# Replicating the attention values through a scratch in memory: one store and four loads a tile in place of sixteen transfers inside SBUF

## The chip, the core and the metric

One core of one Trainium2 chip runs the whole kernel. The metric is device time in microseconds (us). The engines are named as in the profile: PE (TensorE, matrix products), PEld (its weight loads), DVE (VectorE), ACT (ScalarE), POOL (GpSimd), and SP (SyncE), which here only issues the transfers between the chip's memory and SBUF.

## What is computed

One transformer layer over 32 sequences of 512 tokens of width 256, in float32. The part that matters here is the attention: 16 query heads share 4 key/value heads of 64 columns, and every query sees the 128 newest keys.

```
q, k, v = x @ wq.T, x @ wk.T, x @ wv.T        # x normalised; 16, 4 and 4 heads of 64
q, k = rmsnorm(q, q_norm_w), rmsnorm(k, k_norm_w)
scores = einsum('bqhd,bkhd->bhqk', q, k) / sqrt(64)
mask = (i >= j) & (i - j < 128)
y = einsum('bhqk,bkhd->bqhd', softmax(where(mask, scores, -inf)), v)
x = x + y @ wo.T
x = x + ffn(layernorm(x))                     # dense product plus gated low-rank experts
```

## The kernel before

The 16,384 rows of x are cut into 128 tiles of 128 rows. Every engine runs one unrolled program, a sequence of steps, and in each step it works on several tiles at different stages; semaphores tie the engines together. The order of the work within a step is written out by hand in `step` of each engine.

The path of the values is this. PE projects keys and values of tile T into PSUM (`project_kv`). ACT copies the values, scaled, to `v_own[:, T % 2]`, a buffer of two slots, 128 keys on 128 partitions with 256 columns (`store_v`, L316). SP replicates them (`replicate`, L225): the product of probabilities and values is done on blocks of 32 queries that each sit on their own quarter of the partitions, so each of the four quarters of `v_rep` needs all four blocks of 32 keys. `v_rep` has 16 block slots, four tiles of four blocks. PE reads them in `attend` (L730), two tiles later, in 160 products of 32x64 weights with 128 columns each (less for the first tile of a sequence). `attend(T)` waits at its start for the transposed probabilities of the tile and for the replicas, and for nothing inside. In a step PE does `attend(T - 2)` between two groups of `scores` (L714, 32 products each).

What waits for the replicas: `attend(T)` (semaphore `s_vr[T % 8]`, a count of `REPLICAS` a tile), and `store_v(T + 2)`, which overwrites the slot of `v_own`. What SP itself waits for: `s_v` (the values are stored) and `s_pv` of tile T - 3 (the block slots to be overwritten have been read). SP's program in the loop is: load x of five tiles ahead (L191, after `x1` of tile T - 3), store the finished tile T - 4 (L196, after `ob` is ready), replicate tile T + 1. `xs` holds 8 tiles, `ob` two.

Of the kernel before, what the change touches and what calls it, by code (L numbers as in the profile page):

```python
# [4 lines left out]
F32 = mybir.dt.float32  # L5
# [6 lines left out]
P = 128  # L12
# [3 lines left out]
QDIM, KVDIM = HEADS * HD, KV_HEADS * HD  # L16
# [8 lines left out]
QUARTER = 32  # L25
# [3 lines left out]
RING, DEEP, WIDE = 3, 4, 8  # L29
NORM_BY_ACT = (3,)  # L30

SPAN, BLOCKS = P + QUARTER, P // QUARTER
REPLICAS = 16 * BLOCKS * BLOCKS
MASK_PARTS = 6 * BLOCKS - 1


# [4 lines left out]
def live(t):  # L41
    return 0 <= t < TILES
# [6 lines left out]
def done(t):  # L49

    return max(0, min(t + 1, TILES))


def groups(t, g):

    return KV_HEADS * t + g + 1
# [11 lines left out]
def wait(eng, sem, value):  # L68
    if value > 0:
        eng.wait_ge(sem, value)  # L70
# [11 lines left out]
def layer(nc, x, w_qkv, w_o, w_ffn, w_v, norm_w, out):  # L82
    ctx = ExitStack()
    with ctx:
        def sb(name, shape, dt=F32):
            return ctx.enter_context(nc.sbuf_tensor(name, shape, dt))

        def sem(name):
            return ctx.enter_context(nc.semaphore(name))
# [27 lines left out]
        q_raw = sb("q_raw", [P, 2, HEADS, HD])  # L117
        qT = sb("qT", [P, 2, HEADS // 2, P])
        v_own = sb("v_own", [P, 2, KVDIM])

        v_rep = sb("v_rep", [P, DEEP * BLOCKS, KV_HEADS, HD])
        soft = sb("soft", [P, RING, REP, SPAN])
# [29 lines left out]
        s_xst, s_xmv, s_xve, s_xeps, s_xrstd, s_xt, s_xth, s_xtl = (sem(n) for n in ("x_stats_done", "x_mean_done", "x_var_done", "x_eps_done", "x_rstd_done", "x_transposed", "xT_high", "xT_low"))  # L152
        s_kv, s_q = sem("kv_projected"), [sem(f"q{n}_projected") for n in range(2)]
        s_ksq, s_kms, s_kve, s_kr, s_kn, s_kt, s_kT = (sem(n) for n in ("k_squared", "k_summed", "k_mean_square", "k_rms_done", "k_normed", "k_transposed", "kT_stored"))
        s_v, s_vr = sem("values_stored"), [sem(f"values_replicated{n}") for n in range(WIDE)]
        s_qsq, s_qms, s_qve, s_qr, s_qc, s_qt, s_qT = ([sem(f"q{n}_{what}") for n in range(2)] for what in ("squared", "summed", "mean_square", "rms_done", "copied", "transposed", "T_stored"))
        s_s, s_mm, s_exp, s_rden, s_pn = (sem(n) for n in ("scores_done", "scores_masked", "exp_done", "rden_done", "probs_normed"))
        s_pna = sem("probs_normed_by_act")
# [15 lines left out]
        def plain(n):  # L174
            _w, high, _low, at = WEIGHTS[n]
            _, c, cols = high.shape
            return w_plain[:, at:at + c * cols].rearrange("p (c n) -> p c n", c=c)
# [8 lines left out]
        @block.sync  # L186
        def _(sp):
            def load_x(T):
                if live(T):
                    wait(sp, s_x1, done(T - WIDE))  # L190
                    sp.dma_start(xs[:, T % WIDE], x[T * P:(T + 1) * P, :]).then_inc(s_x[T % WIDE], 16)  # L191

            def store(T):
                if live(T):
                    sp.wait_ge(s_ob, done(T))
                    sp.dma_start(out[T * P:(T + 1) * P, :], ob[:, T % 2]).then_inc(s_st[T % 2], 16)  # L196

            def load_weight(n):
                if n == W_O:
                    for g in range(KV_HEADS):  # L200
                        for c in range(2):
                            sp.dma_start(plain(n)[HD * (g % 2):HD * (g % 2) + HD].rearrange("p (k a c) n -> p k a c n", a=2, c=2)[:, g // 2, :, c],
                                         w_o.rearrange("(g c a d) n -> g c d a n", g=KV_HEADS, a=2, c=2)[g, c]).then_inc(s_w[n], 16)
                else:
                    sp.dma_start(plain(n), WEIGHTS[n][0].rearrange("(c p) n -> p c n", p=P)).then_inc(s_w[n], 16)

            load_x(0)
            load_weight(0)
            load_weight(1)
            load_weight(2)  # L210
            sp.dma_start(nw[:], norm_w).then_inc(s_nwl, 16)
            load_x(1)
            load_x(2)
            for n in range(3, len(WEIGHTS)):
                load_weight(n)
            for T in range(3, WIDE):
                load_x(T)
            def replicate(T):
                if live(T):
                    sp.wait_ge(s_v, done(T))  # L220
                    if live(T - 3):
                        sp.wait_ge(s_pv, done(T - 3))
                    for j in range(BLOCKS):
                        for n in range(BLOCKS):
                            sp.dma_start(v_rep[QUARTER * n:QUARTER * n + QUARTER, (BLOCKS * T + j) % (DEEP * BLOCKS)].rearrange("p g d -> p (g d)"),  # L225
                                         v_own[QUARTER * j:QUARTER * j + QUARTER, T % 2]).then_inc(s_vr[T % WIDE], 16)

            for T in range(-1, TILES + 4):
                if T - 3 >= 0:
                    load_x(T + 5)  # L230
                store(T - 4)
                replicate(T + 1)
            for n in range(2):
                sp.wait_ge(s_st[n], 16 * (TILES // 2))
# [56 lines left out]
        def _(act):  # L291
# [18 lines left out]
            def store_v(T):  # L310
                if live(T):
                    act.wait_ge(s_kv, done(T))
                    act.wait_ge(s_xrstd, done(T))
                    if live(T - 2):
                        act.wait_ge(s_vr[(T - 2) % WIDE], REPLICAS * ((T - 2) // WIDE + 1))
                    nc.scalar.activation(v_own[:, T % 2], ps_kv[:, KVDIM:], ACT.Copy, scale=x_rstd[:, T % DEEP]).then_inc(s_v, 1)  # L316
# [343 lines left out]
        def _(pe):  # L660
# [57 lines left out]
            def attend(T):  # L718

                pe.wait_ge(s_pt, groups(T, KV_HEADS - 1))  # L720
                pe.wait_ge(s_vr[T % WIDE], REPLICAS * (T // WIDE + 1))
                for p in range(2):
# [148 lines left out]
```

## Time and profile before

| | us |
|---|---|
| median of 3 runs | 2232.22 |
| lowest and highest | 2228.25 to 2237.21 |
| the profiled execution | 2228.48 |
| its span from the first instruction to the last | 2226.6 |
| mean granted TensorE clock of the profiled execution | 0.992 |

| engine | busy us | share of the span |
|---|---|---|
| PE | 2078.9 | 93% |
| DVE | 2036.1 | 91% |
| ACT | 1840.6 | 83% |
| POOL | 1162.5 | 52% |

Two engines are busy for over nine tenths of the time, in all slices alike after the start; a tile takes 17.4 us in the mean (2226.6 / 128). The 16 engines that move data (DMA) are busy for about a tenth to a fifth, at 50 GB/s. A row of the profile with "SPq" is a transfer that SP issues: its time is the issue, not the move of the data; "us to landing" is from the issue until the semaphore is set. "issue" as what ended a wait means that the engine waited for nothing that the profile shows.

### The profile page before, as it was taken

Reading aid. Unit: us, or ns where it says so; the run is one execution under the profiler, and the core shown is the slowest. Engines: PE = TensorE matmul, PEld = TensorE weight load, DVE = VectorE, ACT = ScalarE, POOL = GpSimd, SP = SyncE. Lnnn points to the kernel's source line nnn. Section 1 sums busy time; section 2 is a strip of 40 time slices with the busy share of each in tenths; the row PEclk is TensorE's granted clock in tenths of the full one; section 3 lists DMA queues with packets and bytes.
Section 4 is the critical chain, followed back from the end, with each engine's and each line's share of the span. In section 5 each row is a group of like instructions: output and inputs, shape, how many; then the busy total and the mean of one; then the engine's idle time right before and its main releaser. Section 6 shows DMA issues by size and latency. Waiting matters only on the chain.

```text
span 2226.6 us, 108163 instructions
## 1 busy us (share of the span) xinstructions
PE 2078.9 (93%) x42768; PEld 1703.3 (76%) x42768; DVE 2036.1 (91%) x8486; ACT 1840.6 (83%) x6663; POOL 1162.5 (52%) x1036
## 2 busy tenths in 40 slices
PE   7999999999999998999999999999999999999996
PEld 4777777777777777777877777777777877777775
DVE  7999998999999998999999999999999999999995
ACT  6888888888888887888888888888888888888884
POOL 3555554555555555555555555555555555555552
PEclk9999999999999999999999999999999999999998
DMA  3111111111111111111111111111111111111110
GB/s 99 44 51 48 51 52 46 50 49 52 47 49 48 52 48 48 49 51 47 50 54 47 49 50 51 50 48 52 47 50 50 52 49 49 48 51 50 49 43 24
DMA packets 138198, 110.88 MB, mean 50 GB/s; under 512 B 37216, under 2 KB 136928, under 8 KB 137696
## 3 DMA queue, kind: packets, MB, share of 16 engines
q1 hardware_dynamic: 137696, 103.97, 17.1%
q8 instruction: 342, 5.60, 1.1%
q14 instruction: 160, 1.31, 0.2%
HBM read 19.93 MB, written 16.78 MB: 16 GB/s over the span
## 4 chain that ended last, share of the span: by engine, by line
PE 61%; DVE 25%; issue 9%; ACT 4%; DMA 0%; DVEq 0%; POOL 0%; SPq 0%
PE ps_y L730 12%; PE ps_scores L714 10%; DVE soft L498 10%; PE ps_y L662 7%; PE ps_y L663 7%; PE ps_y L664 7%; PE ps_y L668 6%; DVE pT L516 6%; PE ps_f L668 3%; DVE yT_l L522 2%; ACT soft L357 2%; PE ps_e L662 2%; PE ps_e L663 2%; PE ps_e L664 2%; PE ps_f L662 2%
## 5 line engine op out<-in xcount | busy, mean ns | idle before, releaser
L348 ACT ACTIVATE soft<-soft,neg_max 128x160 f32<-128x160 f32 x2048 | 848.7, 419 | 0.2 <-DVE neg_max L498 0.2
L275 POOL TENSOR_TENSOR soft<-soft,rden 128x640 f32<-128x640 f32 x384 | 482.0, 1255 | 393.0 <-DVE rden L505 393.0
L264 POOL TENSOR_TENSOR q_r<-q_ve,minus_half 128x8 f32<-128x8 f32 x256 | 420.4, 1642 | 316.3 <-DVE q_ve L485 303.8
L498 DVE CUSTOM_DVE_ANT_0 soft<-ps_scores,mask_band,q_r 128x160 f32<-128x160 f32 x1536 | 495.8, 378 | 37.6 <-PE ps_scores L714 28.1
L516 DVE STREAM_TRANSPOSE pT<-soft 128x640 f32<-128x640 f32 x512 | 415.7, 831 | 96.5 <-PE ps_y L730 91.6
L714 PE MATMUL ps_scores<-kT,qT 64*32 64x160 f32 (+4 forms) x16384 | 395.0, 286 | 36.9 <-issue 27.9
L730 PE MATMUL ps_y<-pT,v_rep 32*64 32x128 f32 x17920 | 329.7, 275 | 79.1 <-issue 77.5
L348 ACT ACTIVATION_READ_ACCUMULATOR soft<-soft,neg_max 128x1 f32 x2048 | 393.5, 192 | 0.0
L730 PEld LDWEIGHTS ps_y<-pT,v_rep 32*64 32x64 f32 x17920 | 284.4, 130 | 120.9 <-issue 119.1
L714 PEld LDWEIGHTS ps_scores<-kT,qT 64*32 64x32 f32 x16384 | 228.4, 106 | 155.8 <-issue 121.4
L363 ACT ACTIVATE yT_h<-ps_y 128x512 fp32r<-128x512 f32 x256 | 139.1, 595 | 228.1 <-PE ps_y L730 228.1
L662 PE MATMUL ps_y<-wo_h,yT_h 128*128 128x256 f32 x1024 | 301.3, 294 | 2.4 <-DVE yT_l L522 2.4
L258 POOL TENSOR_TENSOR k_r<-k_ve,minus_half 128x4 f32<-128x4 f32 x128 | 129.6, 1012 | 326.1 <-DVE k_ve L466 326.1
L664 PE MATMUL ps_y<-wo_l,yT_h 128*128 128x256 f32 x1024 | 289.3, 282 | 0.0
L663 PE MATMUL ps_y<-wo_h,yT_l 128*128 128x256 f32 x1024 | 289.0, 282 | 0.0
L357 ACT ACTIVATE soft<-soft,rden 128x160 f32<-128x160 f32 x512 | 177.7, 418 | 46.6 <-DVE rden L505 45.6
L662 PE MATMUL ps_y<-wqkv_h,xT_h 128*128 128x512 f32 x512 | 213.0, 416 | 2.0 <-DVE wqkv_l L427 1.6
L662 PEld LDWEIGHTS ps_y<-wo_h,yT_h 128*128 128x128 f32 x1024 | 194.3, 190 | 14.2 <-DVE yT_l L522 3.3
L663 PEld LDWEIGHTS ps_y<-wo_h,yT_l 128*128 128x128 f32 x1024 | 196.0, 191 | 11.5
L664 PE MATMUL ps_y<-wqkv_l,xT_h 128*128 128x512 f32 x512 | 202.4, 395 | 0.0
L663 PE MATMUL ps_y<-wqkv_h,xT_l 128*128 128x512 f32 x512 | 202.0, 395 | 0.0
L664 PEld LDWEIGHTS ps_y<-wo_l,yT_h 128*128 128x128 f32 x1024 | 193.7, 189 | 0.0
(102 smaller groups left out, 4531.8 us busy)
## 6 DMA issues: line engine op xcount, KB each, us to landing
v_rep<-v_own SPq DMA_DIRECT2D x2048, 32.0 KB, 1.9
xs<-x SPq DMA_DIRECT2D x128, 128.0 KB, 2.4
out<-ob SPq DMA_DIRECT2D x128, 128.0 KB, 2.1
w_plain<-w_qkv SPq DMA_DIRECT2D x3, 512.0 KB, 5.5
w_plain<-w_o SPq DMA_DIRECT2D x8, 128.0 KB, 5.9
w_plain<-w_ffn SPq DMA_DIRECT2D x1, 392.0 KB, 7.4
w_plain<-w_v SPq DMA_DIRECT2D x1, 128.0 KB, 6.5
nw<-norm_w SPq DMA_DIRECT2D x1, 1.0 KB, 6.0
```

The costliest lines, as they stand in the source:

```text
L264: pool.tensor_tensor(q_r[:, T % DEEP, c], q_ve[:, T % DEEP, c], minus_half[:, 0:8], ALU.pow).then_inc(s_qr[n], 1)
L275: pool.tensor_tensor(soft[:, r], soft[:, r], rden[:, r].unsqueeze(2).to_broadcast([P, REP, SPAN]), ALU.mult).then_inc(s_pn, 1)
L348: last = nc.scalar.activation(soft[:, r, h], soft[:, r, h], ACT.Exp, bias=neg_max[:, r, h:h + 1], scale=-1.0, accum_out=den[:, r, h:h + 1])
L357: last = nc.scalar.activation(soft[:, r, h], soft[:, r, h], ACT.Copy, scale=rden[:, r, h:h + 1])
L498: last = nc.vector.tensor_tensor_reduce(soft[:, r, h], ps_scores[:, h, 0:SPAN], mask_band[:] if slot(T) else mask_first[:], q_r[:, T % DEE ...
L516: nc.vector.transpose(pT[:, g // 2, :, g % 2].rearrange("p e c k -> p e (c k)"), soft[:, ring(T, g)].rearrange("p (e c) k -> p e (c k)", e ...
L662: nc.tensor.matmul(ps, stat_h, mov_h, start=first, stop=False, skip_group_check=onto_ended)
L663: nc.tensor.matmul(ps, stat_l, mov_h, start=False, stop=False, skip_group_check=onto_ended)
L664: return nc.tensor.matmul(ps, stat_h, mov_l, start=False, stop=last, skip_group_check=onto_ended)
L668: last = nc.tensor.transpose(ps[:, c * P:(c + 1) * P], src[:, c * P:(c + 1) * P], ident[:])
L714: last = nc.tensor.matmul(ps_scores[queries, 2 * half + c, first - begin:SPAN], qT[rows, T % 2, 2 * g + c, queries], kT[rows, g // 2, at + ...
L730: last = nc.tensor.matmul(ps_y[HD * half:HD * half + HD, n, P * p:P * p + P], v_rep[rows, keys, 2 * p + half], pT[rows, p, half, :, :, QUA ...
```

## The change

The values of a tile go from `v_own` to a scratch `values` in the chip's memory, two slots of 128 x 256, by one transfer. SP waits until that has landed (a new semaphore for each slot), then for `s_pv` as before, and issues four loads, one for each quarter of `v_rep`'s partitions, each with all four blocks of keys: 32 partitions, four runs of 256 columns on each. The count that readers wait for is 64 a tile in place of 256. Nothing is changed on the other engines.

```
-REPLICAS = 16 * BLOCKS * BLOCKS
+REPLICAS = 16 * BLOCKS
+        values = nc.dram_tensor("values", [2, P, KVDIM], F32, kind="Internal").ap()
-        s_v, s_vr = sem("values_stored"), [sem(f"values_replicated{n}") for n in range(WIDE)]
+        s_v, s_vd, s_vr = sem("values_stored"), [sem(f"values_in_memory{n}") for n in range(2)], [sem(f"values_replicated{n}") for n in range(WIDE)]
             def replicate(T):
                 if live(T):
                     sp.wait_ge(s_v, done(T))
+                    sp.dma_start(values[T % 2], v_own[:, T % 2]).then_inc(s_vd[T % 2], 16)
+                    sp.wait_ge(s_vd[T % 2], 16 * (T // 2 + 1))
                     if live(T - 3):
                         sp.wait_ge(s_pv, done(T - 3))
-                    for j in range(BLOCKS):
-                        for n in range(BLOCKS):
-                            sp.dma_start(v_rep[QUARTER * n:QUARTER * n + QUARTER, (BLOCKS * T + j) % (DEEP * BLOCKS)].rearrange("p g d -> p (g d)"),
-                                         v_own[QUARTER * j:QUARTER * j + QUARTER, T % 2]).then_inc(s_vr[T % WIDE], 16)
+                    for n in range(BLOCKS):
+                        sp.dma_start(v_rep[QUARTER * n:QUARTER * n + QUARTER, BLOCKS * (T % DEEP):BLOCKS * (T % DEEP) + BLOCKS].rearrange("p j g d -> p j (g d)"),
+                                     values[T % 2].rearrange("(j k) c -> k j c", j=BLOCKS)).then_inc(s_vr[T % WIDE], 16)
```

SP's program before, from the replication of tile 2 to the first store of a result:

```order
L225 DMA v_rep<-v_own 32x256 [waits values_stored]
L225 DMA v_rep<-v_own 32x256 x15
L225 DMA v_rep<-v_own 32x256 [waits pv_done,values_stored]
L225 DMA v_rep<-v_own 32x256 x15
L191 DMA xs<-x 128x256 [waits x1_done]
L225 DMA v_rep<-v_own 32x256 [waits pv_done,values_stored]
L225 DMA v_rep<-v_own 32x256 x15
L191 DMA xs<-x 128x256 [waits x1_done]
L196 DMA out<-ob 128x256 [waits out_ready]
```

The same place in the changed kernel, whose lines have other numbers:

```order
L222 DMA values<-v_own 128x256 [waits values_stored]
L227 DMA v_rep<-values 32x4x256 [waits values_in_memory0]
L227 DMA v_rep<-values 32x4x256 x3
L222 DMA values<-v_own 128x256 [waits values_stored]
L227 DMA v_rep<-values 32x4x256 [waits pv_done,values_in_memory1]
L227 DMA v_rep<-values 32x4x256 x3
L192 DMA xs<-x 128x256 [waits x1_done]
L222 DMA values<-v_own 128x256 [waits values_stored]
L227 DMA v_rep<-values 32x4x256 [waits pv_done,values_in_memory0]
L227 DMA v_rep<-values 32x4x256 x3
L192 DMA xs<-x 128x256 [waits x1_done]
L197 DMA out<-ob 128x256 [waits out_ready]
```

Sixteen rows of work a tile became five, with one more wait inside; the load of x and the store of a result, which stand behind the replication, follow after five transfers in place of sixteen. PE, ACT, DVE and POOL have the same instructions in the same order.

## Rows read from the trace of the kernel before

**Rows 1.** The page: busy time by engine, and the chain that ended last, by engine.

```profile
PE 2078.9 (93%) x42768; PEld 1703.3 (76%) x42768; DVE 2036.1 (91%) x8486; ACT 1840.6 (83%) x6663; POOL 1162.5 (52%) x1036
...
PE 61%; DVE 25%; issue 9%; ACT 4%; DMA 0%; DVEq 0%; POOL 0%; SPq 0%
```

**Rows 2.** Waits of the compute engines: waited for, us in total, times, longest.

```profile
ACT yT_h L363 <- PE ps_y L730: 228.1, 128, 4.0
...
DVE pT L516 <- PE ps_y L730: 91.6, 66, 2.3
PE ps_y L730 <- issue: 77.5, 65, 1.8
...
PE ps_scores L714 <- issue: 27.9, 27, 1.7
```

**Rows 3.** Waits of SP, the same columns.

```profile
SPq L225 <- ACT v_own L316: 513.8, 127, 11.3
SPq L196 <- DVE ob L584: 40.1, 4, 13.0
```

**Rows 4.** SP in order of time, three tiles: start us, us, what, count.

```profile
1003.92 10.85 SPq L225 DMA_DIRECT2D v_rep<-v_own  x16
1014.82 0.59 SPq L191 DMA_DIRECT2D xs<-x  x1
1015.45 1.03 SPq L196 DMA_DIRECT2D out<-ob  x1
1019.85 11.95 SPq L225 DMA_DIRECT2D v_rep<-v_own  x16
...
1037.64 11.58 SPq L225 DMA_DIRECT2D v_rep<-v_own  x16
...
1054.56 6.02 SPq L225 DMA_DIRECT2D v_rep<-v_own  x8
```

**Rows 5.** DMA issues: count, KB each, median us from issue to landing.

```profile
v_rep<-v_own SPq DMA_DIRECT2D x2048, 32.0 KB, 1.9
xs<-x SPq DMA_DIRECT2D x128, 128.0 KB, 2.4
out<-ob SPq DMA_DIRECT2D x128, 128.0 KB, 2.1
```

**Rows 6.** Lines L191, L196 and L225: issue time in ns, min/median/max.

```profile
L191 SPq DMA_DIRECT2D xs<-x x128: 337/581/1632, 0.7 to 2100.4; - x128
...
L196 SPq DMA_DIRECT2D out<-ob x128: 332/431/1564, 94.8 to 2224.4; - x128
...
L225 SPq DMA_DIRECT2D v_rep<-v_own x2048: 507/591/2007, 24.5 to 2182.1; - x187
```

**Rows 7.** PE in order of time: L730 and L714 in two tiles.

```profile
1023.09 2.49 PE L730 MATMUL ps_y<-pT,v_rep 32*64 32x128 f32 x155
1027.09 0.44 PE L730 MATMUL ps_y<-pT,v_rep 32*64 32x128 f32 x5 [1.52 <-issue]
...
1040.88 2.54 PE L730 MATMUL ps_y<-pT,v_rep 32*64 32x128 f32 x160
1043.35 0.59 PE L714 MATMUL ps_scores<-kT,qT 64*32 64x160 f32 x17
1044.93 0.50 PE L714 MATMUL ps_scores<-kT,qT 64*32 64x160 f32 x15 [0.99 <-issue]
```

**Rows 8.** The page: DMA queues: packets, MB, share of 16 engines.

```profile
q1 hardware_dynamic: 137696, 103.97, 17.1%
q8 instruction: 342, 5.60, 1.1%
```

**Rows 9.** Stretches of one tile: busy us and count of each engine, PE clock, DMA share, GB/s.

```profile
1005.00:1010.00 5.00, 4.85 (x158) 3.83 (x156) 4.97 (x20) 4.32 (x15) 4.90 (x5) 1.00 0.21 55
...
1016.00:1017.60 1.60, 1.60 (x14) 1.48 (x12) 1.60 (x8) 1.48 (x5) 0.39 (x1) 1.00 0.58 170
1018.00:1020.80 2.80, 2.71 (x41) 2.13 (x22) 2.77 (x16) 2.80 (x12) 0.50 (x2) 1.00 0.00 0
```

## The prediction, made before the changed kernel ran

> **What bounds the kernel now.** I read four views in this order. First the page's engine totals and its chain: PE is busy 93% of the span and DVE 91%, and the chain that ended last runs 61% on PE, 25% on DVE, and 9% on "issue", that is on nothing the profile can name; DMA and SP's queue have 0% [rows 1]. So no transfer ends the kernel, and the first thing to see is that the 2048 transfers that the change removes are not on the path.
>
> Second the waits. No row among the waits of PE, DVE or ACT names v_rep. The waits that matter are PE's own: in attend (L730) PE sat idle 65 times for 77.5 us, and in scores (L714) 27 times for 27.9 us, both ended by "issue" [rows 2]. That is 92 stalls and 105.4 us, 1.15 us each. Those stalls are handed on: ACT waits for attend in every tile and DVE 66 times [rows 2].
>
> Third, PE in order of time, to see what such a stall is. In one tile PE has done 155 of the 160 products of attend, stops for 1.52 us, and does the last five; in the next tile it stops for 0.99 us inside one group of scores [rows 7]. attend waits for semaphores only at its start, so nothing that another engine does can end a wait between product 155 and 156. What is left is that the instruction itself was not there. The DMA queues of the page support that: a queue named "instruction" moved 342 packets, 5.60 MB, so 16 KB each [rows 8], and PE and PEld together ran 85,536 instructions [rows 1], which is 65 bytes an instruction if this queue feeds PE. From its share, one such packet takes 0.011 x 16 x 2226.6 / 342 = 1.15 us of one DMA engine. attend and scores consist of many very short instructions (155 products, each with its weight load, in 2.49 us: 8 ns an instruction), so here PE eats a block of 250 instructions in some 2 us, faster than one comes.
>
> Fourth, SP in order of time, which also gives the length of a tile. From the first transfer of v_rep in one tile to that in the next: 15.93 us, then 17.79 us, then 16.92 us [rows 4]. The second period holds the stall of 1.52 us and the third that of 0.99 us [rows 7]: 15.93 + 1.52 = 17.45 and 15.93 + 0.99 = 16.92. So a microsecond of such a stall costs about a microsecond of the kernel. This is the one way in which I see traffic on the DMA engines reach the time.
>
> **The change, part by part.** It is summed against the profiled execution: 2226.6 us of span and 1.9 us around it, 2228.48 us; the median shown is 2232.22, 3.7 us above it.
>
> SP's time. Before, 16 issues take 10.85 to 11.95 us a tile [rows 4] (591 ns median each [rows 6]). Afterwards there is one store, like that of a result (431 ns to issue, 2.1 us to landing), a wait for it, and four loads, like those of x (581 ns each) [rows 5, 6]: 2.2 + 4 x 0.58 = 4.5 us, so SP is free 6.5 to 7.5 us earlier in each tile. Gain: nothing, because SP already idles 513.8 us in 127 waits for v_own, one in each tile [rows 3], and on the chain its queue has 0% [rows 1]. If the four-run form of the loads cost twice as long to issue, SP would still finish after 6.9 us, before it did until now.
>
> The replicas' arrival. Before, the last replica of a tile lands 10.9 + 1.9 = 12.8 us or so after v_own is stored [rows 4, 5]; now after 2.2 + 3 x 0.58 + 2.4 = 6.3 us. attend reads them two tiles later, over 32 us on. Gain: nothing, and the new wait of 2.1 us costs nothing either: there are 12.8 us before any reader would see even the old lateness. Behind the waiting SP stand only its own four loads, the load of x for a tile five ahead and the store of a result; x lands long before its use, and the result's buffer has two slots. v_own's slot, too, is needed again only two tiles later. The added wait for pv_done is the old one, and no row shows SP waiting there [rows 3].
>
> Start and end of the kernel. Neither the first attend nor the last waited for replicas (no such row), and the last store of a result, which ends the kernel, starts at 2224.4 us [rows 6], long after the last replication. Nothing.
>
> Volume. 2048 transfers of 32 KB go, 67 MB; 512 of 128 KB carry the same 67 MB, and 128 stores add 16.8 MB. At a DMA share of 17.1% for 104 MB [rows 8] that is some 20% afterwards; room for it there is.
>
> The shape of the traffic. This is the term that can count. Now the replicas trickle: DMA share 0.21 at 55 GB/s for 11 us, then 0.58 at 170 GB/s while x is loaded and a result stored, two transfers of 128 KB in 1.6 us, then nothing [rows 9]. Afterwards there is a store of 128 KB, a gap, and four loads of 128 KB issued 0.58 us apart: 226 GB/s and, scaled from the row of 170, a share of 0.77 for 2.4 us. Where does that burst lie? With the store issued at 0, the first load is issued at 2.2 and the last lands at 6.3 us, so their data move from about 3.3 to 5.8 us. attend begins 3.24 us after the first v_rep transfer (1019.85 to 1023.09, 1037.64 to 1040.88), and the stalls begin at 5.7 and at 6.3 us [rows 4, 7], so that the block that comes late is on its way at about 4 to 6 us. The burst lies on top of exactly the fetches whose lateness costs time, more than half of them by my reckoning.
>
> What it does to a fetch no row shows, so bounds. From below: the traffic of before goes away for the fetches that miss the burst, and if all its share of 0.21 had slowed them, each gains 1.15 x 0.21 = 0.24 us: 92 x 0.24 = -22 us. From above: all 92 lie in the burst and are slowed by the difference of the shares, 1.15 x (0.77 - 0.21) = 0.64 us: +59 us. Between: a fetch is a single packet of 16 KB, so I let it wait for what stands before it on its engine and then run through. A load puts 8 KB on each of 16 engines, half a fetch, up to 0.4 us at 0.77 busy; the mean wait is 0.77 x 0.2 = 0.15 us for those in the burst, against 0.21 x 0.05 = 0.01 us now with 2 KB a transfer. With 60% in the burst: 0.14 x 0.6 = 0.08 us a stall, 92 x 0.08 = +7 us. I take that.
>
> [...]
>
> Sum: 2228.5 + 0 + 0 + 7 = 2235.5, rounded to 2236 us.
>
> **Rivals.**
> (a) The burst bites harder (slower). Place: the fetches of PE's instructions during attend and the scores behind it. Price: at 0.3 us a stall 92 x 0.3 = 28 us, 2256 us; with new stalls where a fetch just came in time before, up to 2280. It decides from 0.16 us a stall on (15 us, 2243). For it: the overlap in time, and a period that takes a stall in full. Against: PE is busy in full through the stretch with share 0.58, 1.60 of 1.60 us [rows 9]; but that stretch has long instructions.
> (b) The fetches get freer (faster). The late ones fall into the gap between store and loads, or the loads read memory while the old transfers read and wrote SBUF. Price: 0.15 us less a stall, 2228.5 - 14 = 2215 us. For it: 11 us of traffic a tile become some 5. Against: the gap, from about 2.2 to 3.3 us, ends before the critical block is fetched.
> (c) SP's path becomes visible: store, wait, loads. It would need more than 20 us of extra latency in a tile; unlikely, 2260 us or more.
> (d) Nothing reaches the time, fetches do not feel the neighbours at all: 2228.5 to 2232 us. This lies in the forecast's own band.
>
> **How the numbers follow.** What a measurement of this kernel can tell from no change is about 0.5%, 11 us: 2221 to 2243 around the median. Forecast with (d): 0.65, its own range 2224 to 2243. Rival (a): 0.21. Rival (b): 0.12. Rival (c): 0.02. So faster 0.12, within 0.5% 0.65, slower 0.23. For 8 in 10 the range takes most of (a) and half of (b): 2218 to 2260.
>
> **What would show it.** SP: four loads of about 0.6 us each, a wait of about 1.7 us for the store, and waits for v_own that grow from 4 us a tile to about 10. No compute engine waits for v_rep. DMA share in slices up a little, in short stretches near 0.75. PE: the same 92 or so stalls ended by "issue" in L730 and L714, with a sum near 105 + 7 us; the difference of the two spans should be close to the difference of these sums. (a) shows as a longer sum or more stalls at the same places; (b) as fewer. The forecast is wrong if these stalls change by more than 12 us, or if a stall of another kind appears.

## The result, and the profile after

| | median us | lowest to highest | runs |
|---|---|---|---|
| before | 2230.64 | 2228.25 to 2237.21 | 4 |
| changed | 2266.26 | 2259.30 to 2271.53 | 4 |

The changed kernel takes 1.0153 times as long (95% interval 1.0117 to 1.0189): 36 us more. The forecast was 2236 us in a range of 2218 to 2260, and "slower" had 0.23. The profiled execution took 2271.53 us, its span is 2269.7 us, 43.1 us more than before. It is the slowest of its four executions, and the profiled one of before (2228.48 us) lies at the lower end of its own, which is why the two traces lie 43 us apart and the medians 36.

SP and the transfers first. The page's DMA issues of the changed kernel (count, KB each, us to landing), answering to [rows 5]:

```profile
v_rep<-values SPq DMA_DIRECT2D x512, 128.0 KB, 2.7
xs<-x SPq DMA_DIRECT2D x128, 128.0 KB, 3.7
values<-v_own SPq DMA_DIRECT2D x128, 128.0 KB, 1.7
out<-ob SPq DMA_DIRECT2D x128, 128.0 KB, 1.8
```

The waits of SP, answering to [rows 3]:

```profile
SPq L222 <- ACT v_own L318: 1403.4, 128, 14.2
SPq L197 <- DVE ob L586: 263.0, 128, 15.3
SPq L227 <- DMA values<-v_own: 175.0, 128, 2.0
```

And SP in order of time, answering to [rows 4]:

```profile
1006.14 0.32 SPq L222 DMA_DIRECT2D values<-v_own  x1
1008.08 1.74 SPq L227 DMA_DIRECT2D v_rep<-values  x4
1009.87 0.44 SPq L192 DMA_DIRECT2D xs<-x  x1
1012.20 0.36 SPq L197 DMA_DIRECT2D out<-ob  x1
```

SP does what was forecast, only faster: it waits 1.4 us for the store (175.0 / 128), issues four loads in 1.74 us (0.44 us each; I had 0.58), and waits 11 us a tile for the next values where it waited 4. No compute engine waits for v_rep. What I had not followed to its end: the load of x, which stood 10.9 us behind the first transfer of the values, now stands 3.7 us behind it, right at the tail of the burst, and lands after 3.7 us in place of 2.4.

Then PE. The rows of its waits that answer to [rows 2]:

```profile
ACT yT_h L365 <- PE ps_y L732: 240.5, 128, 4.0
...
DVE pT L518 <- PE ps_y L732: 105.4, 64, 2.7
PE ps_y L732 <- issue: 89.0, 63, 2.2
DVE soft L500 <- PE ps_scores L716: 67.3, 78, 2.3
...
PE ps_scores L716 <- issue: 39.5, 29, 2.1
```

It is the same 92 stalls (63 + 29; before 65 + 27), but 128.5 us in place of 105.4: 1.40 us each in place of 1.15. The stalls are handed on as before, to DVE above all. That they are waits for instructions can be counted: in the trace all 92 lie whole multiples of 256 instructions of PE (its sequencer's counted in) and PEld apart (two of them off by one), and each of the 342 packets of the instruction queue is 16 KB, which is 64 bytes for each of 256. The stretches that answer to [rows 9] show where the burst lies:

```profile
1009.00:1012.60 3.60, 2.80 (x177) 2.37 (x164) 2.86 (x13) 1.81 (x9) 3.36 (x3) 1.00 0.72 187
1012.80:1014.50 1.70, 1.54 (x38) 1.15 (x38) 1.05 (x3) 1.24 (x3) 0.19 (x1) 1.00 0.27 89
1014.60:1022.00 7.40, 7.40 (x102) 6.07 (x100) 7.40 (x32) 6.99 (x28) 3.23 (x3) 1.00 0.01 2
```

A share of 0.72 (estimated: 0.77) for 3.6 us, and in just this stretch PE runs attend and has its stall:

```profile
1009.28 2.52 PE L732 MATMUL ps_y<-pT,v_rep 32*64 32x128 f32 x159
1012.96 0.26 PE L732 MATMUL ps_y<-pT,v_rep 32*64 32x128 f32 x1 [1.16 <-issue]
```

The longer stalls, 23.1 us, make only half of the 43 us. The second part is TensorE's clock. The core's row, before and changed:

```profile
core 0: 2226.6 us, clock 0.992
```

```profile
core 0: 2269.7 us, clock 0.984
```

The traces of all 13 kernels record two levels of it, 1.00 and 0.50 of full speed. So a granted clock of 0.992 means 2 x 0.008 x 2226.6 = 36 us at the lower one, and 0.984 means 73 us. One stretch at the lower level, in the changed kernel, with what PE did before it (first PE in order of time, then the stretches):

```profile
577.71 0.45 PE L732 MATMUL ps_y<-pT,v_rep 32*64 32x128 f32 x7 [1.76 <-issue]
```

```profile
570.00:575.00 5.00, 4.93 (x158) 4.22 (x163) 4.97 (x22) 4.80 (x18) 3.98 (x4) 1.00 0.45 131
575.00:577.70 2.70, 0.95 (x67) 0.73 (x53) 1.27 (x6) 0.00 (x0) 1.56 (x2) 1.00 0.40 103
577.90:581.30 3.40, 3.40 (x46) 2.64 (x43) 2.68 (x11) 2.32 (x8) 1.26 (x1) 0.52 0.02 5
581.40:590.00 8.60, 8.60 (x107) 7.00 (x107) 7.93 (x37) 7.97 (x31) 2.27 (x2) 1.00 0.01 2
```

PE was busy 0.95 of 2.70 us, and the next 3.4 us have a clock of 0.52. Between 100 and 2190 us the changed kernel has 15 such stretches and the kernel before two. Each of the 17 follows, within 1.7 us, one of the longer stalls in attend or scores, of 1.45 to 2.23 us. Most such stalls are followed by none: in the same stretch of time the changed kernel has 45 of 1.45 us or more and the kernel before 23, and 15 and 2 of them have such a stretch behind them. So a long stall does not bring it by itself.

From the trace's records of single packets: the fetches of PE's instructions that end in a stall took about as long as before (1.17 against 1.16 us in the mean), and PE went on as long after a fetch's end (1.40 and 1.39 us); but the packet began 1.17 us before PE ran dry, where it had begun 1.40 us before. A stall is the fetch, plus the time to going on, less that lead: 1.16 + 1.39 - 1.40 = 1.15 us before and 1.17 + 1.40 - 1.17 = 1.40 us now. So nearly all of the quarter of a microsecond by which a stall is longer is the later start of its fetch.

Within the changed kernel the same records tell the fetches apart. Of the 92, 56 began after two microseconds in which the transfers of SP's queue had kept the DMA engines over half busy; their stalls are 1.60 us in the mean, the other 36 are 1.08 us. In the kernel before, in e6 and in e9 below no such fetch has that much traffic ahead of it; e8 and e5 show the same split as the changed kernel (1.48 against 1.12 us, 1.62 against 1.10).

### The profile page after: what moved, and what is told of

Read it like the earlier page. It is cut to its first block, busy times and chain, and to the rows that moved or that the text cites. A ratio compares the mean times of both kernels' runs of the same rounds, so it can differ in the third digit from the quotient of the medians.

```text
span 2269.7 us, 106755 instructions
## 1 busy us (share of the span) xinstructions
PE 2095.5 (92%) x42768; PEld 1715.8 (76%) x42768; DVE 2038.7 (90%) x8486; ACT 1844.7 (81%) x6663; POOL 1162.5 (51%) x1036
## 3 DMA queue, kind: packets, MB, share of 16 engines
q1 hardware_dynamic: 131552, 120.65, 18.4%
## 4 chain that ended last, share of the span: by engine, by line
PE 62%; DVE 23%; issue 10%; ACT 4%; DMA 0%; DVEq 0%; POOL 0%; SPq 0%
PE ps_y L732 12%; PE ps_scores L716 10%; DVE soft L500 9%; PE ps_y L664 7%; PE ps_y L665 7%; PE ps_y L666 7%; PE ps_y L670 6%; DVE pT L518 5%; PE ps_f L670 3%; DVE yT_l L524 2%; ACT soft L359 2%; PE ps_e L664 2%; PE ps_e L665 2%; PE ps_f L664 2%; PE ps_e L666 2%
## 5 line engine op out<-in xcount | busy, mean ns | idle before, releaser
L518 DVE STREAM_TRANSPOSE pT<-soft 128x640 f32<-128x640 f32 x512 | 415.7, 831 | 110.2 <-PE ps_y L732 105.4
```

Of the source, the lines that this page charges most:

```text
L518: nc.vector.transpose(pT[:, g // 2, :, g % 2].rearrange("p e c k -> p e (c k)"), soft[:, ring(T, g)].rearrange("p (e c) k -> p e (c k)", e ...
```

## The experiments

The theory after the result: the four loads, 128 KB each and 0.44 us apart, stand in the DMA engines ahead of a fetch of PE's instructions just where PE is short of them; the later start lengthens the stall, and a longer stall is more often followed by a stretch at half clock. Rivals: reading the chip's memory is what slows the fetches; the size of one transfer, whatever the rate; the wait and the order on SP. All ratios are against the kernel before on the same chip. The last two columns are of one profiled execution each.

| kernel | ratio (95%) | median us | before there | PE waits for issue, L730 + L714, us | clock |
|---|---|---|---|---|---|
| before | 1 | 2230.64 | | 105.4 | 0.992 |
| changed | 1.0153 (1.0117 to 1.0189) | 2266.26 | 2230.64 | 128.5 | 0.984 |
| e1: sixteen loads from memory | 0.9949 (0.9930 to 0.9968) | 2210.86 | 2223.68 | 89.1 | 0.995 |
| e2: burst, late | 0.9947 (0.9929 to 0.9964) | 2209.80 | 2223.68 | 91.5 | 0.993 |
| e3: no replicas | 0.9968 (0.9950 to 0.9985) | 2213.85 | 2223.68 | 97.7 | 0.994 |
| e4: SBUF transfers, late | 0.9947 (0.9928 to 0.9966) | 2210.63 | 2223.68 | 90.8 | 0.995 |
| e8: changed, x late | 1.0122 (1.0083 to 1.0160) | 2252.30 | 2226.24 | 118.2 | 0.990 |
| e5: changed, loads twice | 1.0180 (1.0141 to 1.0220) | 2268.01 | 2226.24 | 130.8 | 0.985 |
| e6: eight loads of 64 KB | 0.9962 (0.9945 to 0.9980) | 2219.04 | 2226.24 | 98.3 | 0.994 |
| e7: store added to before | 0.9976 (0.9959 to 0.9993) | 2221.39 | 2226.24 | 108.1 | 0.995 |
| e9: changed, loads one by one | 0.9950 (0.9934 to 0.9966) | 2214.98 | 2225.19 | 94.1 | 0.993 |
| e1 again | 0.9929 (0.9906 to 0.9953) | 2209.68 | 2225.19 | 95.3 | 0.994 |
| e7 again | 0.9966 (0.9949 to 0.9983) | 2219.64 | 2225.19 | 100.2 | 0.995 |

**e1, the shape of the traffic.** Same store, same wait, same bytes read from memory, in sixteen loads.

```
-                    for n in range(BLOCKS):
-                        sp.dma_start(v_rep[QUARTER * n:QUARTER * n + QUARTER, BLOCKS * (T % DEEP):BLOCKS * (T % DEEP) + BLOCKS].rearrange("p j g d -> p j (g d)"),
-                                     values[T % 2].rearrange("(j k) c -> k j c", j=BLOCKS)).then_inc(s_vr[T % WIDE], 16)
+                    for j in range(BLOCKS):
+                        for n in range(BLOCKS):
+                            sp.dma_start(v_rep[QUARTER * n:QUARTER * n + QUARTER, (BLOCKS * T + j) % (DEEP * BLOCKS)].rearrange("p g d -> p (g d)"),
+                                         values[T % 2, QUARTER * j:QUARTER * j + QUARTER]).then_inc(s_vr[T % WIDE], 16)
```

> The store to memory and the wait stay, but the replicas are made by sixteen loads of 32 KB from the scratch, issued over some 11 us, in place of four of 128 KB. Theory 1, the burst: what costs time is that a load of 128 KB puts 8 KB on each DMA engine ahead of the fetches of PE's instructions. Then the trickle brings back nearly all: 2228 to 2240 us, stalls of PE ended by issue in attend and scores near 105 us. Rival, the memory: reads of the chip's memory slow the fetches whatever their size (the same 67 MB are read): 2255 to 2270 us, stalls near 128 us.

0.9949: not only is the loss gone, it is faster than before, and 2211 us lies below both ranges. Its waits:

```profile
PE ps_y L733 <- issue: 65.6, 65, 1.7
...
PE ps_scores L717 <- issue: 23.5, 24, 1.5
```

Reading memory as such is refuted as the cause of the loss, and so are the store, SP's new wait and the added volume (120.75 MB in this kernel, 120.65 in the changed one).

**e2, the place.** The four loads as changed, but after the store of the result.

```
 for T in range(-1, TILES + 4):
+    store(T - 4)
     if T - 3 >= 0:
         load_x(T + 5)
-    store(T - 4)
-    replicate(T + 1)
+    replicate(T)
```

> The changed kernel, with SP's work in another order: in each turn first the store of the result (which waits for ob, about 6 us after v_own is stored), then the load of x, then store and loads of the values, so that all bursts move after attend and the scores behind it have been fetched. Theory 1, the burst at that place: the stalls are no longer than before the change or shorter, 2205 to 2235 us. Rival, the memory or the added volume wherever it lies: 2255 to 2270 us.

0.9947. The burst of 128 KB loads is in this kernel whole; only it starts some 7 us later in the tile, past attend and the scores behind it. SP in order of time:

```profile
1016.34 0.36 SPq L197 DMA_DIRECT2D out<-ob  x1
1016.74 0.43 SPq L192 DMA_DIRECT2D xs<-x  x1
1017.21 0.45 SPq L222 DMA_DIRECT2D values<-v_own  x1
1019.27 2.08 SPq L227 DMA_DIRECT2D v_rep<-values  x4
```

and its waits:

```profile
PE ps_y L732 <- issue: 67.6, 66, 1.7
...
PE ps_scores L716 <- issue: 23.9, 25, 1.6
```

The same 91 stalls, 1.01 us each. So the place decides: the burst costs 36 us there and nothing that shows here.

**e3, no replicas at all** after the fourth tile (part of the attention is computed from old values).

> The kernel before, with the values replicated for the first four tiles only; later tiles read the old replicas, so part of the computation is left out. It shows what the stalls are with no replica traffic at all. Theory 1: some 92 stalls remain, each at most a little shorter (the trickle put 2 KB on an engine at a time): 2215 to 2232 us, stalls 92 to 105 us. Rival, that the old traffic had lengthened the fetches by its whole share of 0.21: 2205 to 2210 us. Rival, that the stalls are not fetches but something of the data: they vanish, under 2150 us.

0.9968, with 90 stalls of 97.7 us in all. The stalls do not come from the replicas; they are the kernel's own, and traffic only lengthens them. It is no floor, though, and e2 and e4 are below it. With nothing else to do SP loads x early, 4 us before the store of a result:

```profile
1015.10 0.33 SPq L191 DMA_DIRECT2D xs<-x  x1
1019.08 0.34 SPq L196 DMA_DIRECT2D out<-ob  x1
```

Where this load of 128 KB moves its data the critical fetches lie too; that this is the difference to e4 was not tried.

**e4, the old transfers, late.** The edit of e2 on the kernel before.

> The kernel before with its sixteen transfers inside SBUF, in the late order of the second kernel of this set (store of the result, load of x, replicas). Theory 1: the trickle leaves the place of the critical fetches and costs nothing elsewhere: the time of the kernel without replicas, 2215 to 2232 us. Rival, place does not matter: 2228 to 2237 us, as before; a result of the third kernel near before would leave the two alike.

0.9947, 13 us less than before there and 4 us below the range of theory 1: the old trickle, too, had cost something by lying where it lay. "Place does not matter" is out. The load of x has no part in it: nine in ten of the critical fetches of the kernel before start 3.1 to 5.6 us after v_own is stored, and x is issued 11.7 us after it in that kernel and 6.5 us after it here.

**e8, only x moved** out of the burst: `store(T - 4)`, then `load_x(T + 5)`, then `replicate(T + 1)`.

> The changed kernel with the load of x moved behind the store of the result, so that it leaves the critical place (in the changed kernel it follows the four loads directly, at 3.7 us after the store to memory, and lands in 3.7 us where it took 2.4). The four loads stay where they are. If the four loads alone make the fetches late: 2250 to 2265 us. If the load of x, pulled into the same burst, is half of it: 2235 to 2248 us.

1.0122 against 1.0153: by the times the four loads alone make most of the loss, and x's part is some 0.3%, with intervals that overlap. The stalls give x more: 118.2 us, with 128.5 for the changed kernel and 105.4 before, so nearly half of the excess went with x. But the profiled execution of e8 was the fastest of its four and that of the changed kernel the slowest. Between a fifth and a half, the size of x's part stays open.

**e5, twice the loads**, the second four into a spare tile.

> The changed kernel with each of its four loads issued a second time into a spare tile right behind, a burst of 1 MB in place of 512 KB; the load of x moves 1.7 us later. Theory 1, a fetch waits for what is queued on its engine: more of the critical fetches fall into the burst (it now lasts until 8 us after the store), the start of each is as late as now or later, so more than the present 36 us over the kernel before: 2275 to 2320 us, stalls 140 us and up, more stretches at half clock. Rival, that the excess comes from the wait and the order on SP and not from volume: 2260 to 2270 us, as now.

1.0180: above 1.0153 but with overlapping intervals, and 2268 us lies below what the theory had expected and within the rival's range; its stalls (130.8 us, expected 140 and up) and its 12 stretches at half clock (expected more than the 15) are misses of the theory too. The share of the 16 engines rose from 18.4% to 30.1% with hardly an effect. The burst grows only at its end, 5 us and more after the store, where few of the critical fetches start (in the changed kernel four in five have started by then). So it does not tell the theory from its rival, which e1 refutes; it shows once more that volume is not the measure.

**e6, eight loads of 64 KB.**

> The changed kernel with eight loads of 64 KB in place of four of 128 KB: the same bytes from memory at the same place, 4 KB an engine at a time, issued over about 3.5 to 4.6 us in place of 1.7. Between sixteen loads (2211 us, stalls 89 us) and four (2266 us, stalls 128 us). Theory 1, the lateness grows with what one transfer queues on an engine and with the share: 2220 to 2245 us. Rival, any burst faster than the old trickle costs in full: 2255 to 2270 us.

0.9962, 2219 us: just under the theory's range, well under the rival's. With halved transfers the whole loss is gone. SP:

```profile
1011.30 4.82 SPq L229 DMA_DIRECT2D v_rep<-values  x8
```

0.60 us each, so 512 KB in 4.8 us against 1.74 us. Size and rate changed together here; the next one parts them.

**e9, full size, low rate.**

```
 for n in range(BLOCKS):
+    if n:
+        sp.wait_ge(s_vr[T % WIDE], REPLICAS * (T // WIDE) + 16 * n)
      sp.dma_start(v_rep[QUARTER * n:QUARTER * n + QUARTER, BLOCKS * (T % DEEP):BLOCKS * (T % DEEP) + BLOCKS].rearrange("p j g d -> p j (g d)"),
```

> The changed kernel with each of the four loads issued only when the one before it has landed: still 128 KB and 8 KB an engine in each transfer, but one in about 3 us, so half or less of the share, and 12 us in all, the old trickle's length. [...] If what counts is that transfers queue up behind each other faster than the engines drain them: the lateness goes, 2208 to 2222 us, like eight loads of 64 KB (2219).

0.9950. Its waits, SP's four loads, and their time to landing:

```profile
PE ps_y L734 <- issue: 68.2, 65, 1.5
...
PE ps_scores L718 <- issue: 25.9, 28, 1.8
```

```profile
1016.67 7.74 SPq L229 DMA_DIRECT2D v_rep<-values  x4
```

```profile
v_rep<-values SPq DMA_DIRECT2D x512, 128.0 KB, 2.2
```

These loads of 128 KB start at the critical place, 2.4 us apart, and cost nothing that shows. Many of the critical fetches fall between two loads; but 24 of the 93 began right behind traffic, with the DMA engines over half busy in the half microsecond before, and their stalls are 0.91 us in the mean, the others' 1.05. So a fetch is not seen to suffer from what one transfer puts on its engine; it starts late where SP issues several transfers faster than they drain. In the changed kernel a load is issued every 0.44 us, 131 KB / 0.44 us = 298 GB/s, while the engines moved 187 GB/s in that stretch; a load lands after 2.7 us where it takes 2.2 by itself, and the load of x behind the four after 3.7 us where it took 2.4. That is a backlog. The theory as I had it before e9, that the lateness grows with what one transfer puts on an engine, falls; that it comes with the backlog of several stands. No run separates the backlog itself from the high share of busy time that goes with it, and that a fetch waits in the backlog is argued from its later start.

**e7, the source of the reads.** The kernel before with the store and the wait added; the sixteen transfers still read SBUF.

> The kernel before with the store to memory and the wait for it put ahead of its sixteen transfers inside SBUF, which still read v_own: nothing reads the scratch. It differs from the first experiment (2211 us) only in where the sixteen transfers read. If the source matters (reads of SBUF lengthen the fetches, from 1.05 to 1.15 us each): 2222 to 2234 us, as the kernel before. If the start 2 us later is what helped the first experiment: 2208 to 2216 us.

> The store to memory and sixteen loads of 32 KB from the scratch once more, beside its twin below on one chip. 0.994 to 0.996 of the kernel before, fetches of 1.05 us.

> The same with the sixteen transfers reading v_own in SBUF. If the source of the reads counts by itself: 0.997 to 0.999 of the kernel before, with an interval clear of its twin's, and fetches near 1.15 us. If the two first results differed by chip and chance: the same ratio as the twin.

0.9976, and beside its twin 0.9966 (0.9949 to 0.9983) against 0.9929 (0.9906 to 0.9953): both times the kernel that reads memory is about 0.3% faster than the one that reads SBUF, but the intervals overlap, where a clear difference had been expected of the twins. The critical fetches took 1.05 and 1.07 us with the one, 1.15 and 1.11 us with the other. I take it as likely, not as shown. e7 itself is a little faster than before, with one store more; its trickle starts 2 us later, but its stalls (108.1 and 100.2 us against 105.4) do not show that this is the reason, so it stays open.

**Both parts in one sum.** Over the 13 profiles a straight fit gives span = 2101.8 + 1.06 x (PE's wait for issue in attend and scores) + 0.44 x (us at half clock, 2 x (1 - clock) x span), and no span is off by more than 4.2 us. By it the 23.1 us of longer stalls make 24 us and the 37 us more at half clock make 16 us of the 43.1. Stalls and half clock rise together in these runs, so the split leans on few of them: fitted without the changed kernel it still gives 2269.8 us for it (measured 2269.7), but without the changed kernel and e5 it misses both by 7 to 8 us, with 0.29 in place of 0.44.

The two traces themselves settle it better. PE's program is the same in both, so each tile of the changed kernel has its twin: the time from its first product of attend to that of the next tile. Over 118 such periods in a row, which leave out the start and the end, the changed kernel is 43.1 us longer, with 23.8 us more of stalls and 44.4 us more at half clock, and the two differences are hardly tied (correlation 0.25). A straight fit over the 118 gives 1.13 us for a microsecond of stall (standard error 0.03) and 0.40 us for one at half clock (0.01): 27 and 18 us. The 15 periods with a stretch at half clock that their twins lack are 1.4 us longer than their stalls account for. So what half clock costs is measured; that the longer stalls bring it on is argued from the order of the two.

## Why the prediction was wrong

**What bounds the kernel: right.** The stalls that the profile calls "issue" were the one way in which traffic could reach the time, and a microsecond of them costs about one (1.06 in the fit over the kernels, 1.13 tile by tile).

**SP, the replicas' arrival, start and end, volume: right**, at nothing. The loads were issued faster than supposed (0.44 us, not 0.58), and the burst kept the DMA engines 0.7 to 0.9 busy for some 2.4 us, as dense as estimated (0.77).

**The place of the burst: right.** e2 is its proof, and the 60% of the fetches that I had put into it agree with the 56 of 92 that began behind two microseconds of heavy traffic.

**The step that failed: "the mean wait is 0.77 x 0.2 = 0.15 us for those in the burst ... 0.08 us a stall, 92 x 0.08 = +7 us".** Measured: 23.1 / 92 = 0.25 us a stall, three times as much. I let a fetch wait for half of one transfer's part on its engine. The part itself agrees with the trace, where a load of the changed kernel is 128 packets of 1 KB and 16 of 4 bytes, so 8 KB for each of 16 in the mean. The wait was an assumption of mine that no run shows: in e9 there is none to be seen; what costs is four transfers issued 0.44 us apart, where a load takes 2.7 us to land and the load of x behind them 3.7. I had taken two transfers' 170 GB/s [rows 9] and scaled it to a share of 0.77, as if a share below one left no queue.

In the changed kernel a fetch starts 0.23 us later in the mean (1.17 us before PE runs dry, against 1.40). Where in the path it waits, no run shows.

**The term that was missing: the clock.** The sum has no term for it; it is 16 of the 43 us by the fit over the kernels and 18 tile by tile. The profile before had two such stretches behind stalls of 1.45 and 1.73 us, and I had looked only at the mean clock. A long stall can be paid for twice, as the one of 1.76 us above seems to have been.

**The rivals.** (a), the burst bites harder, was the right one, mechanism and place; its price of 28 us for 0.3 us a stall lacked the clock, which is why its 2256 us lies under the measured 2266. Its chance of 0.21 was too small, and the range, cut at 2260, too: the stated upper bound of +59 us stood in the text and the range took half of it. The argument I had put against it (PE busy 1.60 of 1.60 us at a share of 0.58) came, as said there, from a stretch with long instructions, and so was no argument. (b), stalls get shorter, is a real effect, worth some 0.5%, but only where the transfers lie elsewhere (e2, e4) or come thinner (e1, e9). (c) did not happen.

**The threshold.** "The forecast is wrong if these stalls change by more than 12 us": they changed by 23.

## A version that beats both

e1, e2, e4 and e9 all run at about 0.995 of the kernel before and so 2% under the changed one; e1 (sixteen loads from memory) had 0.9949 and 0.9929, but the intervals of all four overlap, so none is shown to be the best. e4 gets as much with no scratch at all, by the order of three lines on SP. The gain over the kernel before is half a per cent, clear of the noise and no more.

## What to carry to other kernels

Transfers on nobody's path still reached the time here, through the fetch of PE's own instructions. Here PE runs 155 very short products in 2.49 us [rows 7], and its instruction stream was late by itself (92 stalls in the kernel before, 90 with no replicas at all); where a trace shows such stalls, see which transfers lie there, and move them or issue them no faster than they drain. Coalescing relieved the issuing queue, which was idle anyway (513.8 us of waits for v_own before), and made the loads come so fast, 0.44 us apart, that the fetches started 0.23 us later. And count a stall of PE once for its length and again where a stretch at half clock follows it (0.40 us for each microsecond of that here).

## What the runs showed that I had not expected

- Four loads of 128 KB issued 0.44 us apart cost 36 us; the same four one after another, 2.4 us apart, cost nothing, and that kernel is faster than the one before (0.9950).
- Each stretch at half clock in the middle of the two kernels came behind one of PE's longer stalls (1.45 to 2.23 us) and cost 0.40 us (tile by tile) to 0.44 us (over the kernels) for each microsecond it lasted.
- Sixteen small transfers that read SBUF, lying where the fetches are, seem to lengthen the fetch of PE's instructions (1.11 to 1.16 us) where sixteen from memory do not (1.05 to 1.07 us).
- A block of PE's instructions arrives, and PE goes on only 1.4 us later (1.38 to 1.45 in the mean), in every kernel of this study.
